# Cross attention and a ternary FFN: other times for GpSimd's looks, and the first input behind two quarters of K's operands

## What is computed

```python
tgt = layernorm(x)
k, v = split((ctx @ W_src.T + b_src) * mask); q = (tgt @ W_tgt.T + b_tgt) * mask
attn = softmax(where(mask == 0, -inf, q @ k.T / sqrt(32)))
x = x + concat(tgt, attn @ v) @ W_out.T + b_out
n = layernorm(x)
h = silu(n @ w1.T * s1) * (n @ w2.T * s2)
h = gelu(h @ h1.T * s); h = gelu(h @ h2.T * s)
out = x + h @ w3.T * s3
```

## Time and profile before

| what | value |
|---|---|
| runs | 916.91, 918.54, 919.99 us |
| profiled execution | 919.11 us, span 917.3 us |
| PE busy | 908.2 us (99%) |
| DVE, ACT, POOL busy | 615.9, 390.8, 76.5 us |
| granted TensorE clock, mean | 0.998 |
| DMA | 79.19 MB, the first two of 40 slices at 351 and 372 GB/s |

### The profile page before, as it was taken

The page is one execution under the profiler, slowest core; times in us unless marked ns, Lnnn a source line. Parts: engine busy times, 40 slices in busy tenths (PEclk is TensorE's granted clock), DMA queues, the critical chain, the costliest instruction groups (busy, mean ns, idle before and its releaser), DMA issues.

```text
span 917.3 us, 20845 instructions
## 1 busy us (share of the span) xinstructions
PE 908.2 (99%) x7600; PEld 866.5 (94%) x7600; DVE 615.9 (67%) x1224; ACT 390.8 (43%) x1100; POOL 76.5 (8%) x101
## 2 busy tenths in 40 slices
PE   9999999999999999999999999999999999999998
PEld 7789999999999999999999999999999999999998
DVE  5886757677585775748767576675857858576453
ACT  6872623425244343533525235252352534455231
POOL 4254001010000100001000010100101000000000
PEclk9999999999999999999999999999999999999999
DMA  9922132311323122132221323213231122203000
GB/s 351 372 86 72 35 122 70 111 44 52 102 69 120 46 74 85 52 120 57 82 77 41 120 69 97 57 34 120 69 120 42 60 87 69 91 23 105 24 13 13
DMA packets 82347, 79.19 MB, mean 86 GB/s; under 512 B 8592, under 2 KB 74896, under 8 KB 82320
## 3 DMA queue, kind: packets, MB, share of 16 engines
q1 hardware_dynamic: 81744, 78.31, 26.5%
q10 hardware_dynamic: 576, 0.52, 0.2%
HBM read 51.55 MB, written 27.26 MB: 86 GB/s over the span
## 4 chain that ended last, share of the span: by engine, by line
PE 94%; DMA 2%; DVE 2%; SPq 1%; issue 1%; ACT 0%; POOL 0%; DVEq 0%; ACTq 0%
PE F L619 56%; PE G L619 7%; PE F L730 7%; PE G L612 6%; PE G L471 6%; PE G L506 5%; PE G L489 2%; PE G L595 2%; PE S L523 2%; DMA hBh_raw<-ctx_t 1%; DMA p_dram<-pb 1%; SPq L335 0%; SPq L386 0%; DVE g L1226 0%; DMA pr<-p_dram 0%
## 5 line engine op out<-in xcount | busy, mean ns | idle before, releaser
L619 PE MATMUL F<-hBh,H 128*128 128x256 f32 x1008 | 240.1, 282 | 0.1
L844 ACT ACTIVATE g<-F,firsts 128x256 f32<-128x256 f32 x250 | 104.6, 471 | 316.4 <-PE F L619 316.2
L619 PE MATMUL F<-hBl,H 128*128 128x256 f32 x1008 | 237.2, 280 | 0.0
L619 PE MATMUL F<-hAh,H 128*128 128x256 f32 x992 | 235.1, 281 | 0.2 <-issue 0.2
L619 PE MATMUL F<-hAl,H 128*128 128x256 f32 x992 | 233.4, 279 | 0.0
L619 PEld LDWEIGHTS F<-hBl,H 128*128 128x128 f32 x1008 | 189.9, 188 | 0.4
L619 PEld LDWEIGHTS F<-hBh,H 128*128 128x128 f32 x1008 | 189.1, 188 | 0.6 <-ACT g L844 0.3
L619 PEld LDWEIGHTS F<-hAh,H 128*128 128x128 f32 x992 | 186.2, 188 | 2.3 <-ACT sil L837 0.4
L619 PEld LDWEIGHTS F<-hAl,H 128*128 128x128 f32 x992 | 186.6, 188 | 0.0
L1245 DVE CAST hBh<-g 128x512 fp32r<-128x512 f32 x64 | 28.1, 439 | 140.8 <-ACT g L844 140.8
L872 ACT ACTIVATE pr<-pr,nmx 128x128 f32<-128x128 f32 x240 | 92.7, 387 | 1.1 <-DVE nmx L1080 0.9
(11 more groups left out here) (160 smaller groups left out, 1504.6 us busy)
## 6 DMA issues: line engine op xcount, KB each, us to landing
p_dram<-pb SPq DMA_DIRECT2D x30, 512.0 KB, 3.4
pr<-p_dram SPq DMA_DIRECT2D x120, 128.0 KB, 2.5
H_raw<-h SPq DMA_DIRECT2D x16, 512.0 KB, 11.7
cT<-ctx_t SPq DMA_DIRECT2D x14, 512.0 KB, 3.4
x_dram<-xt SPq DMA_DIRECT2D x28, 256.0 KB, 2.3
out<-y SPq DMA_DIRECT2D x32, 128.0 KB, 1.7
x_in<-x_t SPq DMA_DIRECT2D x15, 256.0 KB, 2.7
x2T<-x_dram SPq DMA_DIRECT2D x60, 64.0 KB, 1.9
```

What stands on the lines that cost most here:

```text
L619: return mm(bank, W[0][:, k, cols], part[:, k, :], start=first, stop=last)
L844: fn(g[:, q % 2, m, :], mid_bank(f, q)[:, m, :], ACT.Gelu, scale=scols[:, col:col + 1]).then_inc(gelu_ready, 1)
```

## The change

WARM goes from 8 to 6. x of tile 0 is issued behind the second quarter of context 0. The order of the loads behind it is new: context 1 behind chunk 2, seconds behind chunk 3, WO behind chunk 4, x and mask 1 behind WO, context 2 behind chunk 13, the mask row last. GpSimd looks at chunks 3, 9 and 12: the first behind the first kT of tile 1, the second behind the cast of chunk 7, the third behind the first h of the FFN; its casts, sum_low_bits and add_bias(0) have other places too. ScalarE has three looks ahead of the exps. TensorE's attention of tile 0 stands in front of the branch, with other places for the halves of V and Q of tile 1. VectorE copies p's first half a step earlier, does count and flag later, and ln1_apply(2) behind mask_scores(1, 0). SP writes both halves of p before it reads either, in all tiles. Lines of context are cut to the one in front of each edit.

```diff
--- before.py
+++ after.py
@@ -20,7 +20,7 @@
...
 EARLY = 2 * KD
-WARM = 8
+WARM = 6
@@ -268,7 +268,7 @@
...
         assert len(chunks) == CHUNKS
-        on_pool = [18, 19]
+        on_pool = [3, 9, 12]
@@ -327,9 +327,11 @@
...
 
-            def turn_p(a, j):
+            def write_p(a, j):
...
                 sp.dma_start(p_dram[j].rearrange("s p n -> p s n"), pb[j][:]).then_inc(p_written[j], 16)
+
+            def read_p(a, j):
@@ -369,8 +371,10 @@
...
                 if a is not None:
-                    turn_p(a, 0)
-                    turn_p(a, 1)
+                    write_p(a, 0)
+                    write_p(a, 1)
+                    read_p(a, 0)
+                    read_p(a, 1)
@@ -385,24 +389,28 @@
...
 
-            sp.dma_start(x_in[:], x[0]).then_inc(x_loaded, 16)
...
                 sp.dma_start(cT[:, k, :], ctxT[0][:, k * T:(k + 1) * T]).then_inc(k_step_loaded[k], 16)
+                if k == 1:
+                    sp.dma_start(x_in[:], x[0]).then_inc(x_loaded, 16)
...
             sp.dma_start(WV[:], wvT).then_inc(wv_loaded, 16)
-            load_chunks(range(EARLY + 1))
+            load_chunks(range(3))
             sp.dma_start(cT_1.rearrange("p k t -> p (k t)"), ctxT[1]).then_inc(ctx_loaded_1, 16)
+            load_chunks(range(3, EARLY))
+            sp.dma_start(seconds[:], second_rows).then_inc(seconds_loaded, 16)
+            load_chunks(range(EARLY, EARLY + 1))
+            sp.dma_start(WO[:], woT).then_inc(wo_loaded, 16)
             sp.dma_start(tile1_home[:, KC:KC + NB * D // T + 1, :].rearrange("p k t -> p (k t)"), x_mask_1).then_inc(x_loaded_1, 16)
-            sp.dma_start(WO[:], woT).then_inc(wo_loaded, 16)
-            sp.dma_start(seconds[:], second_rows).then_inc(seconds_loaded, 16)
-            load_chunks(range(EARLY + 1, EARLY + 6))
+            load_chunks(range(EARLY + 1, EARLY + 5))
             load_x(2)
-            load_chunks(range(EARLY + 6, EARLY + KH))
+            load_chunks(range(EARLY + 5, EARLY + KH))
             sp.wait_ge(v_done, at("v_done", 0, 1))
+            load_chunks(range(EARLY + KH, EARLY + KH + 2))
             sp.dma_start(cT[:], ctxT[2]).then_inc(ctx_loaded, 16)
+            load_chunks(range(EARLY + KH + 2, CHUNKS))
             load_mask_row(2)
-            load_chunks(range(EARLY + KH, CHUNKS))
@@ -472,7 +480,7 @@
...
 
-            def project_q(a):
+            def project_q(a, cs=range(KD)):
@@ -482,7 +490,7 @@
...
                     pe.wait_ge(ptV_ready, 2)
-                for c in range(KD):
+                for c in cs:
@@ -492,7 +500,8 @@
...
                         ins.then_inc(q_first_done, 1)
-                ins.then_inc(q_done, 1)
+                if cs[-1] == KD - 1:
+                    ins.then_inc(q_done, 1)
@@ -762,9 +771,10 @@
...
 
-            def first_gates(general):
+            def first_attention():
...
                 transpose_p_0(0, (0, 1))
+                project_v(1, [0])
@@ -774,11 +784,11 @@
...
                 out_proj_u_0(1)
+                project_v(1, [1])
                 transpose_x2_0(0)
-                project_v(1, [1])
+                project_q(1, [0])
                 transpose_x2_0(1)
-                project_q(1)
-                gates_part(0, 1, 2, general)
+                project_q(1, [1])
@@ -802,12 +812,12 @@
...
             project_k(1, 1)
-            project_v(1, [0])
+            first_attention()
...
                 pe.wait_ge(chunk_cast, EARLY)
-                first_gates(False)
+                gates_part(0, 1, 2, False)
@@ -817,7 +827,7 @@
...
                 pe.wait_ge(raw_loaded, 32)
-                first_gates(True)
+                gates_part(0, 1, 2, True)
@@ -938,10 +948,10 @@
...
                     if first:
-                        look((on_act[12:13], on_act[13:15], [], [])[q])
+                        look((on_act[10:11], on_act[11:13], [], [])[q])
...
                     copy_xnT(2)
-                    look(on_act[15:])
+                    look(on_act[13:])
@@ -967,23 +977,23 @@
...
             keep_xnT(0)
-            look(on_act[:5])
+            look(on_act[:3])
...
             exps_0(1)
-            look(on_act[5:7])
+            look(on_act[3:4])
             copy_pT_0(0)
-            look(on_act[7:8])
...
             copy_pT_0(1)
-            look(on_act[8:10])
+            look(on_act[4:6])
             copy_upd_0(1)
+            look(on_act[6:7])
...
             x2_hi_0(0)
-            look(on_act[10:11])
+            look(on_act[7:9])
             x2_hi_0(1)
-            look(on_act[11:12])
+            look(on_act[9:10])
@@ -1273,12 +1283,11 @@
...
                 keep_residual(f)
-                if first:
-                    ln1_apply(2)
...
                     mask_scores(1, 0)
+                    ln1_apply(2)
@@ -1354,23 +1363,23 @@
...
             mask_max_0(0, 1)
-            count_low_bits(0, EARLY)
             mask_max_0(1, 0)
-            raise_flag(0)
...
             normalise_0(0)
+            copy_pT_0(0)
             normalise_0(1)
-            copy_pT_0(0)
...
             residual_ln2_stats_0(0)
+            count_low_bits(0, EARLY)
...
             residual_ln2_stats_0(1)
+            raise_flag(0)
@@ -1448,24 +1457,29 @@
...
             mask_bv()
-            for n in range(EARLY):
+            for n in range(EARLY - 1):
                 cast(n)
+            add_bias(0)
+            pool.wait_ge(kT_ready, at("kT_ready", 1, 1))
+            look(on_pool[0])
+            cast(EARLY - 1)
+            inverse_std1(1)
+            cast(EARLY)
+            inverse_std2_0(0)
             sum_low_bits(0)
-            add_bias(0)
-            inverse_std1(1)
-            inverse_std2_0(0)
+            cast(EARLY + 1)
             inverse_std2_0(1)
-            inverse_std1(2)
-            for n in on_pool:
-                look(n)
-            pool.wait_ge(h_ready, at("h_ready", 0, 1))
-            for n in range(EARLY, EARLY + 2):
-                cast(n)
-            pool.wait_ge(h_ready, at("h_ready", 0, 2))
...
                 cast(n)
+            look(on_pool[1])
+            inverse_std1(2)
+            pool.wait_ge(h_ready, at("h_ready", 0, 1))
+            look(on_pool[2])
+            pool.wait_ge(h_ready, at("h_ready", 0, 2))
+            for n in range(EARLY + 4, EARLY + 6):
+                cast(n)
             pool.wait_ge(h_ready, at("h_ready", 0, 4))
-            for n in range(EARLY + 4, EARLY + KH):
+            for n in range(EARLY + 6, EARLY + KH):
```

## The result

The change makes the kernel slower: 922.21 us median of 22 runs (918.99 to 924.85) against 918.75 for the kernel before in the same rounds (22 runs, 916.91 to 923.14), a ratio of 1.0030 with a 95% interval of 1.0021 to 1.0040. The ratio makes it 2.8 us slower, with an interval of 1.9 to 3.7 us; the two medians as they stand are 3.5 us apart. It is above the forecast's own range (915.8 to 919) and above the wider one (914.6 to 920.0).

The account below looks back on a forecast made before the run. TensorE, busy 99% of the span, was taken as the bound. Opening gains and losses left -0.8 us at V(2), -1.3 with attend(1): 919.11 to 917.8 us, 917.2 on the median's footing; own range 915.8 to 919, 80% 914.6 to 920.0.

Parts of the forecast that it names:

- The forecast (4): Whole kernel: the summed steps give 917.2 us on the median's footing, called "same"; chance 0.50.
- Rival (3): Behind TensorE's 1.2 us wait for xn the clock is at 1.2 GHz; 4.5 us lost, 921.7 us; chance 0.10.
- Start: Opening: K starts at 4.23 us, x lands later, transposes of x at 8.5 instead of 7.70: +0.8 us, at most 1.5.
- The clock: Granted TensorE clock behind the opening's wait for xn: no loss in the sum, a fall only as a rival.
- -1.66 us: At project_k(2): with its 2.01 us stall reduced the clock stays up, so its records take 3.72 us, not 5.38.
- Tile 1's context and the softmax: Opening: no wait for context 1, -0.2 us; TensorE waits 0.7 us for p, second transposes at 25.3: -0.5 us.
- Look at chunk 3 and the casts: Before the gates: GpSimd's look and casts hold VectorE; gates at 37.6 us, range 36.9 to 38.3: +1.3 us.
- Gates to project_k(2): 9.56 us of work plus 0.7 of waits, so project_k(2) starts at 47.9, level with 47.86.
- V(2) and attend(1): V(2) waits for kT(2) and starts at 54.0, -0.8 us net; attend(1)'s wait goes, -1.3 us in all.
- The loop: Behind 76 us: the new order of p's writes and reads costs nothing, no waits of its own.

Follow-up runs that it names:

- e4: Changed kernel plus 8 unused filler products on TensorE between K's second quarter and the transposes of x: 920.04 us, ratio 1.0014 to the kernel before.
- f1: Changed kernel with the first two quarters of context 0 loaded as one 256 KB transfer: 918.57 us, ratio 0.9997 to the kernel before.
- f3: e1 with GpSimd's casts (and one sum_low_bits) held until VectorE's normalised rows are ready: 915.20 us, ratio 0.9965 to the kernel before.
- e1: Changed kernel with x again the first load and 8 warm-up products, all else kept: 917.73 us, ratio 0.9985 to the kernel before.
- g2: Kernel before with its two GpSimd looks (chunks 18 and 19) given to ScalarE, nothing else: 919.43 us, ratio 0.9997 to the kernel before.
- g3: f3 with SP reading p's first half back before writing the second, as the kernel before does: 917.54 us, ratio 0.9988 to the kernel before.
- g1: Changed kernel, x still third, with GpSimd's casts held behind VectorE's normalised rows: 920.07 us, ratio 1.0004 to the kernel before.
- e3: Kernel before with only the two start edits, x behind two quarters of context 0 and 6 warm-up products: 921.70 us, ratio 1.0031.
- h2: f1 with the first two quarters of WK also in one load: 918.35 us, ratio 1.0006 to the kernel before.
- f2: Changed kernel with x behind one quarter of context 0 instead of two: 917.59 us, ratio 0.9990 to the kernel before.

## Why the prediction was wrong

The forecast (4), "same" at 917.2 us, failed at one step above all: when x lands. Rival (3), slower by the clock, which I had given 0.10, came true in its direction, but its mechanism is only a part: e4 puts the clock at 1.5 us of the 4.1 that the start costs. That its 921.7 us lies near the measured 922.21 is luck. It took 0.8 us for x's lateness (2.9 in the profiled execution), 1.3 for the way to the gates (2.8) and 4.5 for the clock behind x's wait (2.4). Step by step:

**Start: this step failed.** I took x's landing from the transfer that stood third in the queue before, "the same 512 KB up to its end", 3.9 us behind its issue. It took 5.9 (5.5, 5.1 and 4.9 in the other three kernels with two quarters in front). Equal bytes ahead were not an equal time, since the bytes ahead were different transfers: the throughput at 3 to 5 us was 205 and 142 GB/s, not 368 and 379. The term of +0.8 us is +2.9 in the profiled execution, and my upper bound of 1.5 was too small as well, and no row stood behind it. The same mistake has another side. I took WK's landing from the old order too, 3.5 us and K at 4.23; it took 2.6, and K started at 3.77. Its first half ended at 6.55, not at 7.3, which bought nothing, because the transposes behind it need x: it made the wait longer. Of the 4.07 us of waiting against the 1.2 of the sum, 2.1 are xn's lateness and 0.8 K's earliness.

**The clock.** The forecast had none of it. Rival (3) had the place right (behind the wait for xn) and the direction; its price of 4.5 us was too high, the profiled execution lost 2.4 us there. Its "against", that 0.98 us of idle had not lowered the clock, was a row about a shorter gap than the one at issue. A wait of 1.2 us might indeed have passed: 1.55 us in e4 and 1.73 in f1 were followed by 1.00. The decisive error was the length of the wait.

A second error is in the base. The -1.66 us for the clock behind the old stall was read from one execution, at 0.998; 72 of 108 runs of the kernel before read 1.000, so in most of them there was no such fall to win back. I brought the execution's 919.11 down to the median by 0.57 us and left the 1.66 in full.

**Tile 1's context and the softmax: right.** No wait for context 1. From project_k(1) to the second transposes of p it was 29.79 - 22.08 = 7.7 us, 7.7 forecast, with a wait for p of 0.56 us (0.7 forecast).

**Look at chunk 3 and the casts: mechanism right, size too small.** mask_bias(1) was held for 1.45 us. For the casts I took the middle between held and not held; all three products were held, by 0.68, 0.97 and 0.69 us. From the second transposes to the gates: 13.3 us, 12.3 forecast. The row I set against a hold (mbias at 55.87, unstretched) was an operation that GpSimd doesn't release, in the midst of a run of four casts (from 53.91 for 4.13 us); why that one wasn't held stays open. f3 gives the price of the held products, 1.8 us of time. And the 1.8 us wait in front of the gates, which I had not named as a risk to the clock, brought it down in this execution: 1.4 us more.

**Gates to project_k(2): right in the profiled execution.** 10.97 us, less 1.4 us for the low clock at the gates, is 9.6: I had 9.56 and 0.7 of waits, and the waits didn't come, since everything was late enough. project_k(2) took 3.69 us at 1.00. e1 has neither the stall nor the low clock there either, and g2 shows that the two looks caused the stall.

**V(2) and attend(1): right.** 6.2 us from project_k(2) to V(2) with a wait for kT(2) of 0.77 us; forecast 6.1. No wait at attend(1). g3 says that the new order of p is needed for it (0.8 us of wait without).

**The loop**: 0.3 us of a wait for p behind 84 us where I had none.

With the start undone, the forecast's other steps give a check: the change without x's lateness (+0.8) would have been 916.4, a ratio of 0.9977 to the 918.54 that the forecast started from. e1 measured 0.9985, 0.8 us above and inside its interval: the rest of the forecast agrees within the noise, though the casts' held products and the base of the -1.66 us were not.

What stays open is why the transfers dip with two short quarters in front of x, and what decides whether the clock falls behind a wait of 1.8 us. x on another queue was not tried, nor the new order of the later loads by itself.

## What to carry to other kernels

- The landing of whatever stood in a place of a DMA queue before is no bound for what is moved there: 3.9 us from the issue before, 4.9 to 5.9 with other transfers in front. Ask what stands in front of it now, on this queue and on the others. And where the moved operand is the second thing that TensorE needs, starting the first thing sooner gained nothing.
- A step on GpSimd that is queued right behind the value for which VectorE waits can stretch VectorE's use of it, as it did in all three places here. A wait for VectorE's product in front of it cost little and gained (f3 over e1, 1.8 us of 918; g1 over the change, 2.4).
- Taking one stall away is worth what the chain behind it allows: g2 took 2 us of stall away at 46 us and found a wait and a low clock of the same size at 73. And read the mean clock of each run beside its time, before a single profile is taken for the median; that goes for the kernel before as well.

## What the runs showed of the hardware that was not expected

- **The clock behind short waits differs from run to run.** Wait on TensorE and granted clock that followed: 4.07 us (the change), 3.11 (g1), 2.43 and 2.17 (e3), 2.01 (before) and 1.95 (g2), 0.50 each time; 1.8 us, 0.50 in four executions and 1.00 in four; 1.73 (f1), 1.60 (h2) and 1.55 us (e4), 1.00. The 2.01 us of before aren't followed by a fall in most of its runs either, by their mean clock (72 of 108 at 1.000). Over 22 runs of one program the mean clock goes from 0.994 to 1.000 and the time by 5.9 us with it.
- **Eight float32 products of zeros, and the clock stayed up**: 1.95 us of filler in the 3.5 us gap (e4), 1.00 behind it, and 9 of 11 runs at 1.000 where the change has 3 of 22.
- **The clock's column doesn't show the start**: it reads 1.00 in the first microseconds, beside warm-up products that leave 12 records in 2.93 us, while 16 records of the same product take 1.95 us in e4. In f2 the transposes of x, at 8.56 us and 1.00, take 1.06 us for 0.60.
- **A VectorE product released by GpSimd was stretched by what GpSimd had queued next**: three products for which GpSimd's power releases VectorE took 1.42, 1.38 and 1.10 us, beside the cast behind that power (for the second, sum_low_bits' reduction and then the cast), and within 0.01 us the same in all eight executions with this order. With the casts held back they took 0.74, 0.41 and 0.41. The Trainium skill (SBUF — State Buffer, "SBUF: two separate sides") has the exclusive lock; that the releasing engine's next instructions won it each time is what these rows add.
- **A load at the very start of the program is sensitive to what stands beside it**: 256 KB took 3.0 to 3.5 us in front of all, and 3.7, 4.0, 4.4 and 4.9 to 5.9 us by what was in front of it.
